# Causal masks as the first products of the score banks, in a fused attention and expert kernel on one core

## The reference

```
q, k, v = x @ Wq[h], x @ Wk[h], x @ Wv[h]           # per head h: (256, 64)
scores  = where(causal, q @ k.T / sqrt(64), -inf)   # (256, 256)
attn    = softmax(scores)
heads   = attn @ v
y       = x + concat(heads) @ Wo                    # then a layer norm
```

## Time and profile before

| | us |
|---|---|
| three runs, median (lowest to highest) | 775.23 (774.15 to 779.05) |
| the profiled execution, its own time | 774.88 |
| its span, first to last instruction | 773.1 |
| busy in it: PE | 706.1 (91%) |
| busy: PEld | 600.2 (78%) |
| busy: DVE | 568.0 (73%) |
| busy: ACT | 526.7 (68%) |
| busy: POOL | 293.5 (38%) |

### The profile page before, as it was taken

One profiled execution on the slowest core, in us unless ns is written; L12 is line 12 of the kernel. 1 busy time (PEld: TensorE's weight loads), 2 busy tenths in 40 slices (PEclk: granted clock), 3 DMA queues, 4 the chain that ended last, 5 costly groups with the idle time before them and its releaser, 6 DMA issues.

```text
span 773.1 us, 17658 instructions
## 1 busy us (share of the span) xinstructions
PE 706.1 (91%) x5954; PEld 600.2 (78%) x5955; DVE 568.0 (73%) x1914; ACT 526.7 (68%) x1687; POOL 293.5 (38%) x404
## 2 busy tenths in 40 slices
PE   4999999999999999999999999999977779999954
PEld 3788878888888888888888888878767779999921
DVE  4668888889788888989888888988867444443316
ACT  4877877778778887878778877877754534444506
POOL 3024444232423324232433423241416564555535
PEclk9999999999999999999999999999989999999978
DMA  8530000000000000000000000000021232222155
GB/s 182 173 64 8 8 9 22 15 23 8 22 9 22 19 19 22 8 22 8 22 12 19 23 15 22 8 16 8 16 64 49 57 115 81 70 73 76 46 160 187
DMA packets 43702, 34.88 MB, mean 45 GB/s; under 512 B 10625, under 2 KB 40321, under 8 KB 43617
## 3 DMA queue, kind: packets, MB, share of 16 engines
q1 hardware_dynamic: 37984, 23.81, 11.4%
q0 software_dynamic: 4544, 9.45, 3.4%
q10 hardware_dynamic: 1088, 0.54, 0.2%
HBM read 20.22 MB, written 13.56 MB: 44 GB/s over the span
## 4 chain that ended last, share of the span: by engine, by line
PE 69%; DVE 16%; issue 5%; ACT 3%; POOL 2%; another core or an unknown queue 2%; DVEq 1%; DMA 1%; POOLq 0%; ACTq 0%; SPq 0%
PE PT1O L424 10%; PE A L671 8%; PE SC L407 8%; PE M L386 5%; DVE prob L782 5%; PE PT1O L443 5%; PE M L388 4%; PE SC L415 4%; PE M L387 4%; PE SC L410 3%; PE A L435 3%; DVE pT L790 3%; DVE prob L784 3%; PE SC L386 2%; PE SC L388 2%
## 5 line engine op out<-in xcount | busy, mean ns | idle before, releaser
L1212 ACT ACTIVATE qk<-M 128x512 f32<-128x512 f32 x127 | 75.9, 598 | 93.4 <-PE M L388 93.4
L1223 ACT ACTIVATE prob<-SC,nmax 128x256 f32<-128x256 f32 x256 | 123.4, 482 | 0.0
L1476 POOL DMA_INDIRECT expert_rows<-v_sb,got x78 | 77.4, 992 | 62.2 <-ACT v_sb L1346 33.4
L424 PE MATMUL PT1O<-pT,v_sb 128*64 128x256 f32 (+1 forms) x1024 | 98.6, 335 | 0.1
L424 PEld LDWEIGHTS PT1O<-pT,v_sb 128*64 128x64 f32 x1024 | 64.1, 138 | 42.1 <-issue 17.3
L1217 ACT ACTIVATE prob<-SC,nmax 128x128 f32<-128x128 f32 x256 | 93.7, 372 | 3.6 <-DVE nmax L774 3.6
L782 DVE TENSOR_TENSOR prob<-prob,rden 128x512 f32<-128x512 f32 x128 | 89.3, 698 | 4.4
L1468 POOL DMA_INDIRECT sent_rows<-rec,slot x64 | 70.0, 1094 | 55.2 <-DVE slot L984 37.4
L386 PE MATMUL M<-xt_hi,wqk_hi 128*128 128x256 f32 x254 | 82.5, 325 | 6.2 <-ACT xt_st L1207 4.6
L671 PE MATMUL A<-w_sb,hidT 128*128 x624 | 79.1, 281 | 9.6 <-ACT v_sb L1346 5.9
L774 DVE TENSOR_REDUCE nmax<-SC 128x2 f32<-128x512 f32 x128 | 87.1, 681 | 0.0
(11 more groups left out here) (197 smaller groups left out, 1819.0 us busy)
## 6 DMA issues: line engine op xcount, KB each, us to landing
got<-sent_rows SPq DMA_DIRECT2D x39, 132.0 KB
w_in<-expert_rows SPq DMA_DIRECT2D x16, 256.0 KB, 3.4
x_in<-L_attn_x SPq DMA_DIRECT2D x16, 128.0 KB, 2.0
w_in<-L_ffn_w SPq DMA_DIRECT2D x1, 2048.0 KB, 12.4
x_res<-L_attn_x SPq DMA_DIRECT2D x16, 128.0 KB, 2.2
w_sb<-L_ffn_w SPq DMA_DIRECT2D x8, 256.0 KB, 4.6
out<-y_out SPq DMA_DIRECT2D x8, 256.0 KB, 2.1
sent_rows<-pad_rec SPq DMA_DIRECT2D x11, 132.0 KB, 5.1
```

The costliest lines, as they stand in the source:

```text
L424: last = mm(PT1O[k * E:(k + 1) * E, cols], v_sb[:, t, h * E:(h + 1) * E], src[:, par, k, :], start=(t == 0), stop=(t == 1), skip_group_che ...
L1223: return a.activation(prob[:, slot, k, 1:3, :].rearrange("p n t -> p (n t)"), SC[par][:, k, LATE_Q], ACT.Exp, bias=nmax[:, par, 0, k:k + 1 ...
```

## The change

The masks of a pair are written as the first products of its two banks, with `start=True`; the scores of the later rows, which had that, now add to them, and the last score product raises `s_mm`. In a step `masks(0)` goes ahead of the value sums, behind a wait for `exp_done` p + 1; `masks(1)` goes behind them, with a wait for `exp_done` p + 2; then both scores follow. The number of products and their sizes are as before.

```diff
+            def masks(par):
+                for k in range(2):
+                    mm(SC[par][:, k, P:S + P], ident_bf[:], mask[:].rearrange("p n t -> p (n t)"),
+                       start=True, stop=False, skip_group_check=True)
             def scores(par):
                 for k, r in heads:
-                    mm(SC[par][:, k, LATE_Q], qk[r, par, 0, P:S], qk[r, par, 1, :], start=True, stop=False,
+                    mm(SC[par][:, k, LATE_Q], qk[r, par, 0, P:S], qk[r, par, 1, :], start=False, stop=False,
                        skip_group_check=True)
                 for k, r in heads:
-                    mm(SC[par][:, k, EARLY_Q], qk[r, par, 0, 0:P], qk[r, par, 1, 0:P], start=False, stop=False,
-                       skip_group_check=True)
-            def masks(par):
-                for k in range(2):
-                    last = mm(SC[par][:, k, P:S + P], ident_bf[:], mask[:].rearrange("p n t -> p (n t)"),
-                              start=False, stop=True, skip_group_check=True)
+                    last = mm(SC[par][:, k, EARLY_Q], qk[r, par, 0, 0:P], qk[r, par, 1, 0:P], start=False, stop=True,
+                              skip_group_check=True)
                 last.then_inc(s_mm, 1)
...
             pe.wait_ge(sem("mask_ok"), 1)
+            masks(0)
+            masks(1)
             pe.wait_ge(qk_sb, 1)
             scores(0)
             pe.wait_ge(qk_sb, 2)
             scores(1)
-            masks(0)
-            masks(1)
...
                     v_proj(turn[0], turn[1])
+                if more:
+                    pe.wait_ge(exp_done, p + 1)
+                    masks(0)
                 if k >= 1:
...
                     pv_two((c - 2) % NP)
                 if more:
+                    pe.wait_ge(exp_done, p + 2)
+                    masks(1)
                     pe.wait_ge(qk_sb, p + 4)
-                    pe.wait_ge(exp_done, p + 1)
                     scores(0)
-                    pe.wait_ge(exp_done, p + 2)
                     scores(1)
-                    masks(0)
-                    masks(1)
```

## The result

The changed kernel takes 793.75 us in the median of its runs (791.43 to 794.52), against 776.1 for the kernel before in the same comparison: a ratio of 1.0224, 95% interval 1.0195 to 1.0254. The forecast was 792.5 us, its own range 785 to 799. The profiled execution has a span of 791.3 us, 18.2 more than before.

The account below looks back on a forecast made before the run. PE was taken to bound the attention stage, some 550 of 773 us. From 774.9 us, plus 12.4 for the new change of shape, plus 6.7 for the early wait, minus 1.5 covered by DVE: 792.5 us, range 785 to 799.

Parts of the forecast that it names:

- The fourth change of shape: Scores to the first f32 q and k projection product: 0.20 us in each of 62 steps, 12.4 us slower.
- Rivals 1 and 2: First q/k projection product after scores: only drain paid, 786.3 us, chance 0.14; or nothing paid, 780.1 us, chance 0.11.
- The drain rule as a rival: At the scores-to-projection change only the drain costs, 0.10 us, f32 load hidden or shared: 786.3 us, chance 0.14.
- The early wait: Wait for exp_done p+1 ahead of the first masks and value sums delays PE at u = 2 and 3: 6.7 us.
- The wait for the second exponentials: Wait for exp_done p+2, moved ahead of the second masks: already met when PE asks, cost 0.
- What DVE covers: Where DVE is late, in the last attention steps, PE's loss is covered: 1.5 us back.
- The faster case: Earlier first maximum lets DVE normalise earlier; PE's waits at the transposes go, new shape change free: 756.0 us, chance 0.07.
- The fourth, an ACT that is late in all kinds of step: ACT's signal comes late for the first masks in all four step kinds, 7.5 us more: 800 us, chance 0.11.

Follow-up runs that it names:

- The third run: Kernel before, with one pair's masks ahead of its scores and the other pair's masks last, all behind the value sums: 781.56 us, ratio 1.0091.
- the second run: Changed kernel, but with both pairs' masks written behind the value sums, so no new wait stands ahead of those: 789.53 us, ratio 1.0183 to before.
- the fifth: Kernel before, with the second output projection put ahead of PE's wait before the second transposes, except in steps u = 2: 760.35 us, ratio 0.9794.
- the last run: Like the fifth, but in steps u = 2 the second output projection also moves, ahead of the q and k projection: 761.84 us, ratio 0.9816 to before.
- the sixth: Changed kernel, with the second output projection put ahead of PE's wait before the second transposes, except in steps u = 2: 787.52 us, ratio 1.0146 to before.
- fourth run: Kernel before, with each pair's masks directly behind its own scores, making five changes of shape: 794.24 us, ratio 1.0234.
- in the first: Kernel before, with only the wait for exp_done p+1 moved ahead of the value sums: 777.76 us, ratio 1.0035.
- the moved projection: Second output projection put ahead of PE's wait before the second transposes: 760.35 us in the order of before, 787.52 us in the changed kernel.

## Why the prediction was right

**The fourth change of shape** (12.4 us) was the term that mattered, and its size held. Rivals 1 and 2 would have left the first L386 at 0.22 and at 0.12; it takes 0.32. The price, taken from the scores behind the value sums because no row had the scores ahead of an f32 load, was 0.20 in the chain after. Three runs with other orders bear it out: 0.197 a step with four changes and no early wait, 0.104 with four of which the last is light, 0.287 with five, against 0.20, 0.10 and 0.30.

**The drain rule as a rival.** The third run shows 0.10 for a change with a bf16 load behind it, the changed kernel 0.20 with an f32 one. By the rule of the Trainium skill (TensorEngine Tiling (Array Packing), Key Properties) each change of tiling mode drains the engine. The runs agree that each has a price, but the count of drains alone, each at the 0.10 of the cheap change, would have given half of it.

**The early wait** (6.7) was too large: 3.9 over the regular batches, by the second run. At u = 2 it costs 0.20 to 0.22, not 0.27, and at u = 3 the masks begin 0.29 after the V product, 0.05 late and not 0.11. The step that was off is the delay of the signal: I took 0.11 from L1207, and the masks' load follows L1219's read by 0.05. Step 1 loses another 0.5 there, with its masks 0.74 after the V product. The wait for the second exponentials was met in the regular steps, as forecast: at u = 2 the read ends at 324.83, and the masks' load begins at 325.05.

**The start of the kernel** I had left out. The first value sums begin at 28.05 before and 29.83 after, 1.77 later. ACT's copy of q and k in step 0 already starts 0.46 later (15.86, 16.32). But in the five runs that leave the start as it was this copy starts at 15.13 to 16.20, so the 0.46 is not shown to come from the change. From that copy to the first value sums it is 12.20 before (12.20 in the fifth and the last run too) and 13.51 after (13.49 in the sixth). Of these 1.3 us, 0.64 is lost up to DVE's first copy of transposes, in step 1 (24.75, 25.85): masks that ACT's last exponential releases now stand ahead of the scores. The other 0.67 is in step 1, and the second run, which has no masks ahead of the value sums, has 12.83, without it: about 0.45 is the early wait, and 0.22 the masks themselves. The 0.22 comes back at the end, as the last step has no masks. The chain has the masks there:

```profile
12.28 0.88 PE SC L406 x4
...
22.78 0.39 PE SC L406 x2
```

**What DVE covers** (1.5) was not there as a sum. Steps 11 and 12, in which DVE is late, shrank by 0.18 and 0.05 where others of their kind grew by 0.26 and 0.21, so 0.7 came back. At the end of the attention steps 62 and 63 together grew by 1.03 instead of being covered: step 62 by 1.31, and step 63, whose value sums have no masks ahead, shrank by 0.28. Ahead of step 62 DVE's addition L999 (L1001 now) starts as follows, before and after:

```profile
545.10 0.51 PE L461 MATMUL A<-rw_sb,xfT 128*128 128x8 f32 x4
...
545.72 0.42 DVE L999 TENSOR_TENSOR att<-xn_res,A 128x256 f32<-128x256 f32 x1 [0.64 <-PE A L435]
```

```profile
561.69 0.51 PE L462 MATMUL A<-rw_sb,xfT 128*128 128x8 f32 x4
...
563.76 0.42 DVE L1001 TENSOR_TENSOR att<-xn_res,A 128x256 f32<-128x256 f32 x1 [2.10 <-PE A L462]
```

Before, the addition follows the end of the product by 0.11, as in every batch that has the product. After, the row names L462 as what was waited for, but that had ended at 562.20, 1.56 earlier, so something else holds DVE. All twelve such additions from the fourth to the fifteenth come 1.55 to 1.60 after the end of their product. In the other steps u = 2 the table shows no cost of it. In step 62 DVE is the late engine, and there it fits: in the second, third and fourth run, where the addition is held by 1.3 to 1.5 us, step 62 grew by 1.09, 1.19 and 1.01; in the first, where it follows by 0.11, by 0.01. What holds the addition no trace shows.

**The sum.** 12.4 for the shapes, 3.9 for the wait, 1.77 at the start, 0.7 back in steps 11 and 12, 0.6 more at the end than the shapes explain, and 0.5 less in the 15 steps u = 1, which grew by 0.17 and not 0.20: 17.5 us. The last group of value sums begins 17.84 us later (575.42 to 593.26), and the experts add 0.35. The wait, with step 1, was forecast too large by some 2.3 us; the rest of the start (1.3) and DVE's cover (1.4) were together too small by 2.7. The large term was right by its mechanism; that the total lies within 1.3 us of the forecast is in part luck, as the errors of the small ones nearly cancel.

**The rivals.** The faster case needed DVE's own maxima to hold up the copy of the transposes; they do not: where the maxima come earlier, the wait moves to that copy, as said, and PE's waits for DVE stay. The fourth, an ACT that is late in all kinds of step, is wrong for this kernel, but comes up with a faster PE, as the moved projection shows.

## What to carry to other kernels

When products of different tile shapes share the array, count the changes of shape on the path and look at the product that enters behind each: put a cheap one, here the bf16 masks, or one of the neighbour's shape, at the seam. Before moving a wait ahead of work that did not need it, compare the signal's time with PE's in every kind of step, also for a faster PE: slack that the old order held is what a later gain is paid from. And look for work that is ready and can stand in front of a wait: here that alone was worth 2%.

## What was not expected of the hardware

A gain in one stage came with a lower granted clock in the next: in the last run's profiled execution the attention ended 3.2 us earlier than in the fifth's, and the span was 2.4 us longer (761.4 against 759.0). That the one caused the other is not shown.

DVE's addition L1001 was held 1.55 to 1.60 us beyond the product that the profile names, in one order of PE's work and not in another; as far as the table and step 62 show, it cost time only where DVE was late anyway.

A mask load that needs no change of shape starts only 0.24 after the start of the last V product (313.74, load at 313.98), the time that such a product holds the array, though ACT's read had ended at 313.57. It costs next to nothing, as the load is short. Why it does not lie under the V product was not tried.
